# Row maxima of the attention taken from pairs of PSUM banks, in five groups per head group

## The chip, the cores and the metric

The kernel runs on one core of a Trainium2 chip. The metric is the device time of one execution in microseconds (us), the median of several runs. Engines: PE (TensorE, matrix products), DVE (VectorE), ACT (ScalarE), POOL (GpSimd), SP (SyncE, issues DMAs).

## The reference

The reference is a small network on 4096 tokens (8 sequences of 512) with 256 channels: two convolution-like blocks, an attention (L2), a mixture of experts, a second attention (L3) with rotary positions and gates, and a second mixture of experts. The change touches only the core that both attentions share. In the reference it is, for 16 query heads, 4 key/value heads and a head size of 16:

```python
scores = jnp.einsum('bgrqd,bgkd->bgrqk', qg, k) * SCALE       # r: 4 heads share one k, v
scores = jnp.where(causal, jnp.finfo(scores.dtype).min, scores)
attn = jax.nn.softmax(scores, axis=-1)
out = jnp.einsum('bgrqk,bgkd->bgrqd', attn, v)
```

In L3 the result is also multiplied by a gate per token and head. A softmax subtracts the largest score of each row (query) before the exponential.

## The kernel before

`attention` (from L1171) works through 32 units u per layer, one for each of 8 sequences and 4 key/value heads. A unit has 4 heads of 512 queries by 512 keys, causal, so in blocks of 128 a head has 10 blocks of scores; 4 heads are 40 blocks, or ten PSUM banks of 512 columns. The ten banks are the list `order`, n = 0 to 9, in the kinds A, B, A, B, C, A, B, A, B, C. Each unit passes two times over its scores:

- Maxima, two units ahead. PE computes scores with the queries on the partitions into `ps_m` (`max_unit`, L1299): A is one query block against 512 keys, B one against 384 and one against 128, C two against 256; each piece is a bf16 product (L1310) and a 128x128 product that adds the causal mask (L1312). DVE takes the row maxima (`reduce`, L1436: A at L1443, B at L1445 and L1446, C at L1448). `ps_m` has two banks, n%2, so bank n waits until the maxima of n-2 have been taken (`m_reduced`).
- `turn_tops` (L1331): one PE transpose turns the 16 columns of maxima into `ps_top`; DVE splits them in two bf16 parts (`split_tops`, L1457 and L1459), and SP puts them as two more rows below the queries (`put_tops`, L1243), so that the second product subtracts them.
- Exponentials. PE computes the scores again with the keys on the partitions into the two banks of `ps_t` (`exp_unit`, L1327), bank n waits for the exponential of n-2; ACT takes the exponential (L1403). POOL clears what lies above the diagonal when all ten are there (four selects, L1273).
- `weigh_values` (L1348), one unit later: probabilities by values, in four key blocks kb, into `ps_v`. ACT copies the sums (`copy_out`, L1410). `turn_out` (L1358), another unit later: four transposes into `ps_o`, from which DVE divides by the sum of the row (`normalise`, from L1468; L3 has one multiply by the gate more, L1471).

PE's instructions stand in one order written by hand, in `unit` (L1361). For each n of unit u: `max_unit` of unit u+2, `exp_unit` of unit u; then at n=0 `turn_tops` of u+1, at n=3 (`TURN_AT`) `turn_out` of u-2, and at n = 4, 6, 8, 9 (`WEIGH_AT`) one key block of `weigh_values` of u-1. DVE has its own order in its `unit` (L1479): ten reductions of unit u+2, `split_tops` of u+1 after n=1, `normalise` of u-2 after n=4. Units 0 and 1 have their maxima ahead of all that; units 30 and 31 have none to take for later ones. The eight PSUM banks are `ps_m` 2, `ps_t` 2, `ps_v` 2 (by turns), `ps_o` 1, `ps_top` 1.

Of the kernel before, what the change touches and what calls it, by code (L numbers as in the profile page):

```python
# [15 lines left out]
F32 = mybir.dt.float32  # L16
# [1154 lines left out]
def attention(net, layer, weights, scratch, values, gates, out):  # L1171
# [13 lines left out]
    TURN_AT, WEIGH_AT = 3, (4, 6, 8, 9)  # L1185
    with ExitStack() as ctx:
# [36 lines left out]
        with nc.Block() as block:  # L1223
# [71 lines left out]
            def _(pe):  # L1295
# [3 lines left out]
                def max_unit(u, j, n, first):  # L1299

                    kind, r = order[n]
                    if n == 0:
                        pe.wait_ge(loaded[j], (u - j) * 24 + 96)
                    if not (first and n < 2):
                        pe.wait_ge(m_reduced, u * UN + n - 1)
                    bank = ps_m[:, n % 2, :]
                    pieces = {"A": [(r, 3, 0)], "B": [(r, 2, 0), (r, 0, 3 * P)], "C": [(r, 1, 0), (r + 1, 1, 2 * P)]}
                    for head, qb, at in pieces[kind]:
# [5 lines left out]
                    last.then_inc(m_scored, 1)  # L1314
# [16 lines left out]
                def turn_tops(u, j):  # L1331
                    pe.wait_ge(m_reduced, u * UN + UN)
                    pe.transpose(ps_top[0:GR * TB, 0:P], top[j % 2][:, :, :].rearrange("p h t -> p (h t)"),
                                 net.ident[:, :]).then_inc(top_turned, 1)

                def weigh_values(u, j, kb, first):

                    if kb == 0:
                        pe.wait_ge(probs_ready, u + 1)
                        pe.wait_ge(v_ready, u + 1)  # L1340
                        if not first:
                            pe.wait_ge(oT_ready, u - 1)
                    pr = probs[j % 2]
                    for r in range(GR):
# [3 lines left out]
                        last = pe.matmul(ps_v[32 * r:32 * r + 32, j % 2, kb * P:S], v[j][:, kb, :], src,  # L1348
# [12 lines left out]
                def unit(u, j, maxima=True, tops=True, weigh=True, turn=True, first=False, first_turn=False,  # L1361
# [3 lines left out]
                    for n in range(UN):  # L1365
                        if maxima:
                            max_unit(u + 2, (j + 2) % 4, n, False)
                        exp_unit(u, j, n, first)
                        if n == 0 and tops:
                            turn_tops(u + 1, (j + 1) % 4)  # L1370
                        if n == TURN_AT and turn:
                            turn_out(u - 2, (j + 2) % 4, first_turn)
                        if n in WEIGH_AT and weigh:
                            weigh_values(u - 1, (j + 3) % 4, WEIGH_AT.index(n), first_weigh)
                for u in range(2):
                    for n in range(UN):
                        max_unit(u, u, n, u == 0)
                    if u == 0:
                        turn_tops(0, 0)
                unit(0, 0, weigh=False, turn=False, first=True)  # L1380
                unit(1, 1, turn=False, first_weigh=True)
                unit(2, 2, first_turn=True, first_weigh=True)
# [14 lines left out]
            def _(act):  # L1397
# [8 lines left out]
                def copy_out(u, j, first):  # L1406
# [3 lines left out]
                    act.activation(oT[j % 2][:, :], ps_v[:, j % 2, :], ACT.Copy).then_inc(oT_ready, 1)  # L1410
# [14 lines left out]
            def _(dve):  # L1425
# [10 lines left out]
                def reduce(u, j, n, first):  # L1436
                    kind, r = order[n]
                    if n == 0 and not first:
                        dve.wait_ge(top_turned, u - 1)
                    dve.wait_ge(m_scored, u * UN + n + 1)  # L1440
                    bank, t = ps_m[:, n % 2, :], top[j % 2]
                    if kind == "A":
                        last = dve.tensor_reduce(t[:, r, 3:4], bank, AX.X, ALU.max)  # L1443
                    elif kind == "B":
                        dve.tensor_reduce(t[:, r, 2:3], bank[:, 0:3 * P], AX.X, ALU.max)  # L1445
                        last = dve.tensor_reduce(t[:, r, 0:1], bank[:, 3 * P:4 * P], AX.X, ALU.max)  # L1446
                    else:
                        last = dve.tensor_reduce(t[:, r:r + 2, 1], bank.rearrange("p (h k) -> p h k", h=2),  # L1448
# [1550 lines left out]
```

## Time and profile before

| | |
|---|---|
| Time, 3 runs | 2412.57, 2414.94, 2416.8 us; median 2414.94 |
| Span of the profiled execution | 2414.8 us (the profile gives no other time of it) |
| PE busy | 2096.5 us (87%) |
| DVE busy | 1678.3 us (69%) |
| ACT busy | 1283.7 us (53%) |
| POOL busy | 711.2 us (29%) |
| Attention core of L2, first product to last unit | 387.4 to about 705 us |
| Attention core of L3, first product to last unit | 1464.0 to about 1782 us |

The span runs from the first to the last instruction. A matmul's duration in the trace holds the time in which its result runs through the array after its columns have gone in, so successive matmuls overlap in the rows, and the engine looks busy in small gaps. Where a difference of start times of two rows is used, it is the time that PE needed from one to the other.

### The profile page before, as it was taken

How to read it: one execution, taken by the hardware profiler on the slowest of the kernel's cores; microseconds unless marked ns; L12 is line 12 of the kernel's file. 1: busy time of each engine (PE TensorE's matmuls, PEld its weight loads, DVE VectorE, ACT ScalarE, POOL GpSimd, SP SyncE). 2: the span in 40 equal slices, each digit the busy share in tenths (PEclk: the TensorE clock that was granted, in tenths of full speed). 3: DMA queues.
4: the chain of work that ended last, by engine and by line, in shares of the span. 5: the costliest groups of instructions: out<-in, count | busy, mean ns of one | idle time of the engine just before them, and what ended most of it. 6: DMA issues, size and time to landing. Idle time of an engine off the chain costs nothing. (4 is left out here: it accounts for less than half of the span.)

```text
span 2414.8 us, 45217 instructions
## 1 busy us (share of the span) xinstructions
PE 2096.5 (87%) x15328; PEld 1597.7 (66%) x15328; DVE 1678.3 (69%) x3514; ACT 1283.7 (53%) x2221; POOL 711.2 (29%) x688
## 2 busy tenths in 40 slices
PE   5969777999987899959998467999985499999998
PEld 4758533444445788859998223444454399999998
DVE  2867756888845776636665697888835877777775
ACT  2434443666653444235554233666652088888885
POOL 1423200222220000038887000222210045555553
PEclk7989887999998899969999786999997799999999
DMA  3000033212103000086665342212104367777774
GB/s 123 1 0 0 0 84 101 59 51 56 51 9 108 3 1 1 1 198 117 116 98 70 102 106 75 59 50 56 51 1 110 123 207 220 222 222 223 222 224 97
DMA packets 176774, 218.56 MB, mean 91 GB/s; under 512 B 34057, under 2 KB 152498, under 8 KB 176242
## 3 DMA queue, kind: packets, MB, share of 16 engines
q1 hardware_dynamic: 146290, 175.19, 23.6%
q0 software_dynamic: 30336, 41.44, 10.7%
q8 instruction: 88, 1.44, 0.3%
q14 instruction: 60, 0.49, 0.1%
HBM read 161.25 MB, written 54.79 MB: 89 GB/s over the span
## 5 line engine op out<-in xcount | busy, mean ns | idle before, releaser
L1403 ACT ACTIVATE L_attn_probs<-L_attn_ps_t 128x512 f32<-128x512 f32 x640 | 374.8, 598 | 245.1 <-PE L_attn_ps_t L1327 240.0
L1310 PE MATMUL L_attn_ps_m<-L_attn_k,L_attn_q 96*128 96x512 bf16 (+3 forms) x1024 | 283.4, 316 | 35.3 <-DMA L_attn_k<-L_k_parts 28.7
L1273 POOL TENSOR_SCALAR_AFFINE_SELECT L_attn_probs<-L_attn_probs 128x512 f32<-128x512 f32 x256 | 153.3, 635 | 469.0 <-ACT L_attn_probs L1403 469.0
L1310 PEld LDWEIGHTS L_attn_ps_m<-L_attn_k,L_attn_q 96*128 96x128 bf16 x1024 | 101.8, 99 | 240.6 <-issue 71.8
L1327 PE MATMUL L_attn_ps_t<-L_attn_q,L_attn_k 98*128 98x512 bf16 (+3 forms) x1024 | 245.0, 301 | 2.8 <-ACT L_attn_probs L1403 2.3
L2450 POOL DMA_INDIRECT out<-L_experts_result,L_moe_give x78 | 161.7, 2073 | 208.6 <-DVE L_experts_result L2622 196.8
L1443 DVE TENSOR_REDUCE L_attn_top<-L_attn_ps_m 128x1 f32<-128x512 f32 x256 | 175.3, 685 | 61.8 <-PE L_attn_ps_m L1312 60.6
L1312 PE MATMUL L_attn_ps_m<-L_attn_causal,L_attn_ident 128*128 128x128 bf16 x1024 | 200.6, 227 | 0.0
L1348 PE MATMUL L_attn_ps_v<-L_attn_probs,L_attn_v 128*32 128x512 f32 (+3 forms) x2048 | 191.4, 448 | 3.0 <-POOL L_attn_probs L1273 2.8
L2729 POOL DMA_INDIRECT L_experts_token<-L_moe_rows,L_moe_take x80 | 81.8, 1022 | 377.7 <-POOLq L1766 324.0
L2468 PE MATMUL L_experts_ps_y<-L_experts_w_high,L_experts_hT_low 128*128 128x256 f32 x624 | 179.5, 288 | 0.0
L2468 PE MATMUL L_experts_ps_h<-L_experts_xT_high,L_experts_w_low 128*128 128x256 f32 x624 | 177.8, 285 | 0.0
L2469 PE MATMUL L_experts_ps_h<-L_experts_xT_high,L_experts_w_high 128*128 128x256 f32 x624 | 177.6, 285 | 0.0
L2470 PE MATMUL L_experts_ps_h<-L_experts_xT_low,L_experts_w_high 128*128 128x256 f32 x624 | 177.5, 284 | 0.0
L2470 PE MATMUL L_experts_ps_y<-L_experts_w_low,L_experts_hT_high 128*128 128x256 f32 x624 | 176.4, 283 | 0.0
L2469 PE MATMUL L_experts_ps_y<-L_experts_w_high,L_experts_hT_high 128*128 128x256 f32 x624 | 176.3, 283 | 0.0
L2556 ACT ACTIVATE L_experts_full<-L_experts_ps_h,L_staged_b 128x256 f32<-128x256 f32 x312 | 129.9, 467 | 68.3 <-PE L_experts_ps_h L2470 68.3
L2607 DVE TENSOR_TENSOR L_experts_hT_low<-L_experts_full,L_experts_hT_high 128x512 fp32r<-128x512 f32 x156 | 107.5, 690 | 67.9 <-ACT L_experts_hT_high L2561 42.3
L1445 DVE TENSOR_REDUCE L_attn_top<-L_attn_ps_m 128x1 f32<-128x384 f32 x256 | 140.2, 547 | 3.7 <-PE L_attn_ps_m L1312 2.7
L2438 POOL DMA_INDIRECT L_experts_token<-L_moe_rows,L_moe_take x78 | 90.4, 1160 | 168.2 <-POOLq L1766 144.7
L2739 POOL DMA_INDIRECT L_moe_total<-L_experts_result,L_moe_give x80 | 128.1, 1601 | 37.4 <-DVE L_experts_result L2907 23.9
L2894 DVE TENSOR_TENSOR L_experts_hT_low<-L_experts_full,L_experts_hT_high 128x256 fp32r<-128x256 f32 x160 | 64.5, 424 | 84.8 <-ACT L_experts_hT_high L2854 59.5
(435 smaller groups left out, 6110.5 us busy)
## 6 DMA issues: line engine op xcount, KB each, us to landing
L_staged_w<-L_ffn_w SPq DMA_DIRECT2D x78, 1024.0 KB, 6.6
L_attn_q<-L_q_parts SPq DMA_DIRECT2D x64, 192.0 KB
L_attn_q<-L_q_parts SPq DMA_DIRECT2D x64, 128.0 KB
L_moe_rows<-L_moe_ln_normed SPq DMA_DIRECT2D x16, 512.0 KB, 3.0
L_q_parts<-L_qkv_q_parts SPq DMA_DIRECT2D x32, 192.0 KB, 2.9
L_q_parts<-L_qkv_parts SPq DMA_DIRECT2D x32, 192.0 KB, 3.1
load_ring<-x SPq DMA_DIRECT2D x8, 512.0 KB, 4.2
L_attn_q<-L_q_parts SPq DMA_DIRECT2D x64, 64.0 KB
```

The source lines that it names most:

```text
L1273: return pool.affine_select(out=block, in_=block, compare_op=ALU.is_ge, fill=0.0, base=0, pattern=columns, channel_multiplier=-1)
L1310: pe.matmul(bank[:, at:at + width], q[j][0:96, head, qb * P:(qb + 1) * P], k[j][0:96, 0:width], start=True, stop=False)
L1312: last = pe.matmul(bank[:, at + width - P:at + width], ident16[:, :], causal16[:, :], start=False, stop=True)
L1327: last = pe.matmul(bank[:, at:at + width], k[j][0:98, kb * P:(kb + 1) * P], q[j][0:98, head, kb * P:S], start=True, stop=True)
L1348: last = pe.matmul(ps_v[32 * r:32 * r + 32, j % 2, kb * P:S], v[j][:, kb, :], src, start=kb == 0, stop=kb == TB - 1, tile_position=(0, 32 ...
L1403: act.activation(probs[j % 2][:, place[unit], :], ps_t[:, n % 2, :], ACT.Exp, scale=scale).then_inc(exped, 1)
L1443: last = dve.tensor_reduce(t[:, r, 3:4], bank, AX.X, ALU.max)
L1445: dve.tensor_reduce(t[:, r, 2:3], bank[:, 0:3 * P], AX.X, ALU.max)
L2450: pool.indirect_dma_start(out=total, out_offset=bass.IndirectOffsetOnAxis(ap=tables.give[:, t:t + 1], axis=0), in_=result[t % GIVEN][:, :] ...
L2468: pe.matmul(out, left_low, right_high, start=first, stop=False)
L2469: pe.matmul(out, left_high, right_high, start=False, stop=False)
L2470: return pe.matmul(out, left_high, right_low, start=False, stop=last)
```

## The change

The ten banks of maxima of a unit become five groups of two banks, the list `sweeps`: two A, two B (of heads 0 and 1), two C, two A, two B. `ps_m` has four banks in two pairs, used in turn. PE still scores one bank at each n (`max_bank`: group n//2, half n%2), but asks only at the first half of a group for the maxima of the group before last. DVE has one reduction over both banks for a group of kind A or C and two for kind B: 7 instead of 14 for a unit. The banks come from `ps_v`, which keeps one (so that `weigh_values` waits for the copy of the unit before, `oT_ready` u instead of u-1), and from `ps_top`, which becomes the first 16 partitions of the first quarter of `ps_o`. Since the two share a bank, `turn_tops` waits also for `normalise` (`o_done`), and `turn_out` for `split_tops` (`top_ready`). On PE `turn_tops` moves from n=0 to n=2 and `turn_out` from n=3 to n=5, behind the first key block of `weigh_values` at n=4. On DVE `split_tops` comes after group 1 and `normalise` after group 3.

```diff
+    sweeps = [[[(0, 3, 0)], [(1, 3, 0)]],
+              [[(0, 2, 0), (0, 0, 3 * P)], [(1, 2, 0), (1, 0, 3 * P)]],
+              [[(0, 1, 0), (1, 1, 2 * P)], [(2, 1, 0), (3, 1, 2 * P)]],
+              [[(2, 3, 0)], [(3, 3, 0)]],
+              [[(2, 2, 0), (2, 0, 3 * P)], [(3, 2, 0), (3, 0, 3 * P)]]]
+    SW = len(sweeps)
+    TOPS_AT, TURN_AT, WEIGH_AT = 2, 5, (4, 6, 8, 9)
...
-        ps_m = net.ps(f"{tag}_ps_m", [P, 2, S], F32, ctx)
+        ps_m = net.ps(f"{tag}_ps_m", [P, 2, 2, S], F32, ctx)
         ps_t = net.ps(f"{tag}_ps_t", [P, 2, S], F32, ctx)
-        ps_v = net.ps(f"{tag}_ps_v", [P, 2, S], F32, ctx)
+        ps_v = net.ps(f"{tag}_ps_v", [P, S], F32, ctx)
         ps_o = net.ps(f"{tag}_ps_o", [P, TB, P], F32, ctx)
-        ps_top = net.ps(f"{tag}_ps_top", [P, S], F32, ctx)
+        ps_top = ps_o[0:GR * TB, 0, :]
...
-                def max_unit(u, j, n, first):
-
-                    kind, r = order[n]
-                    if n == 0:
+                def max_bank(u, j, n, half, first):
+
+                    if n == 0 and half == 0:
                         pe.wait_ge(loaded[j], (u - j) * 24 + 96)
-                    if not (first and n < 2):
-                        pe.wait_ge(m_reduced, u * UN + n - 1)
-                    bank = ps_m[:, n % 2, :]
-                    pieces = {"A": [(r, 3, 0)], "B": [(r, 2, 0), (r, 0, 3 * P)], "C": [(r, 1, 0), (r + 1, 1, 2 * P)]}
-                    for head, qb, at in pieces[kind]:
+                    if half == 0 and not (first and n < 2):
+                        pe.wait_ge(m_reduced, u * SW + n - 1)
+                    bank = ps_m[:, (j + n) % 2, half, :]
+                    for head, qb, at in sweeps[n][half]:
                         width = (qb + 1) * P
                         pe.matmul(bank[:, at:at + width], q[j][0:96, head, qb * P:(qb + 1) * P], k[j][0:96, 0:width],
                                   start=True, stop=False)
                         last = pe.matmul(bank[:, at + width - P:at + width], ident16[:, :], causal16[:, :],
                                          start=False, stop=True)
-                    last.then_inc(m_scored, 1)
+                    if half:
+                        last.then_inc(m_scored, 1)
...
-                def turn_tops(u, j):
-                    pe.wait_ge(m_reduced, u * UN + UN)
-                    pe.transpose(ps_top[0:GR * TB, 0:P], top[j % 2][:, :, :].rearrange("p h t -> p (h t)"),
+                def turn_tops(u, j, first):
+
+                    pe.wait_ge(m_reduced, u * SW + SW)
+                    if not first:
+                        pe.wait_ge(o_done, u - 3)
+                    pe.transpose(ps_top, top[j % 2][:, :, :].rearrange("p h t -> p (h t)"),
                                  net.ident[:, :]).then_inc(top_turned, 1)
...
-                            pe.wait_ge(oT_ready, u - 1)
+                            pe.wait_ge(oT_ready, u)
...
-                def turn_out(u, j, first):
+                def turn_out(u, j, tops=True):
+
                     pe.wait_ge(oT_ready, u + 1)
-                    if not first:
+                    if tops:
+                        pe.wait_ge(top_ready, u + 4)
+                    else:
                         pe.wait_ge(o_done, u)
...
-                            max_unit(u + 2, (j + 2) % 4, n, False)
+                            max_bank(u + 2, (j + 2) % 4, n // 2, n % 2, False)
                         exp_unit(u, j, n, first)
-                        if n == 0 and tops:
-                            turn_tops(u + 1, (j + 1) % 4)
+                        if n == TOPS_AT and tops:
+                            turn_tops(u + 1, (j + 1) % 4, first_tops)
                         if n == TURN_AT and turn:
-                            turn_out(u - 2, (j + 2) % 4, first_turn)
+                            turn_out(u - 2, (j + 2) % 4, tops)
                         if n in WEIGH_AT and weigh:
...
                 def reduce(u, j, n, first):
-                    kind, r = order[n]
+
                     if n == 0 and not first:
                         dve.wait_ge(top_turned, u - 1)
-                    dve.wait_ge(m_scored, u * UN + n + 1)
-                    bank, t = ps_m[:, n % 2, :], top[j % 2]
-                    if kind == "A":
-                        last = dve.tensor_reduce(t[:, r, 3:4], bank, AX.X, ALU.max)
-                    elif kind == "B":
-                        dve.tensor_reduce(t[:, r, 2:3], bank[:, 0:3 * P], AX.X, ALU.max)
-                        last = dve.tensor_reduce(t[:, r, 0:1], bank[:, 3 * P:4 * P], AX.X, ALU.max)
+                    dve.wait_ge(m_scored, u * SW + n + 1)
+                    banks, t = ps_m[:, (j + n) % 2, :, :], top[j % 2]
+                    head, block, _ = sweeps[n][0][0]
+                    if block == 3:
+                        last = dve.tensor_reduce(t[:, head:head + 2, 3], banks, AX.X, ALU.max)
+                    elif block == 2:
+                        dve.tensor_reduce(t[:, head:head + 2, 2], banks[:, :, 0:3 * P], AX.X, ALU.max)
+                        last = dve.tensor_reduce(t[:, head:head + 2, 0], banks[:, :, 3 * P:4 * P], AX.X, ALU.max)
                     else:
-                        last = dve.tensor_reduce(t[:, r:r + 2, 1], bank.rearrange("p (h k) -> p h k", h=2),
+                        last = dve.tensor_reduce(t[:, :, 1], banks.rearrange("p b (h k) -> p (b h) k", h=2),
                                                  AX.X, ALU.max)
                     last.then_inc(m_reduced, 1)
...
-                    for n in range(UN):
+                    for n in range(SW):
                         if maxima:
                             reduce(u + 2, (j + 2) % 4, n, False)
                         if n == 1 and tops:
                             split_tops(u + 1, (j + 1) % 4, first_tops)
-                        if n == TURN_AT + 1 and turn:
+                        if n == 3 and turn:
```

## Rows read from the trace of the kernel before

**Rows 1.** Busy time by stretch: length, PE, PEld, DVE, ACT, POOL, granted clock, DMA.

```profile
430.00:680.00 250.00, 248.38 (x2265) 120.45 (x2261) 206.34 (x480) 166.33 (x294) 69.60 (x135) 1.00 0.20 52
```

**Rows 2.** Timeline, PE, turn_tops of units 1 and 29: start us, duration us.

```profile
412.88 0.28 PE L1333 MATMUL L_attn_ps_top<-ident,L_attn_top 128*16 128x128 f32 x1
...
676.48 0.27 PE L1333 MATMUL L_attn_ps_top<-ident,L_attn_top 128*16 128x128 f32 x1
...
1490.17 0.28 PE L1333 MATMUL L_attn_ps_top<-ident,L_attn_top 128*16 128x128 f32 x1
...
1753.76 0.27 PE L1333 MATMUL L_attn_ps_top<-ident,L_attn_top 128*16 128x128 f32 x1
```

**Rows 3.** Timeline, PE, one period of the L2 attention from turn_out on.

```profile
499.64 0.60 PE L1358 MATMUL L_attn_ps_o<-ident,L_attn_oT 128*128 128x128 f32 x4
500.17 0.28 PE L1310 MATMUL L_attn_ps_m<-L_attn_k,L_attn_q 96*128 96x256 bf16 x1
...
500.83 1.06 PE L1348 MATMUL L_attn_ps_v<-L_attn_probs,L_attn_v 128*32 128x512 f32 x8
...
502.12 0.38 PE L1327 MATMUL L_attn_ps_t<-L_attn_q,L_attn_k 98*128 98x512 bf16 x1
502.33 0.33 PE L1310 MATMUL L_attn_ps_m<-L_attn_k,L_attn_q 96*128 96x384 bf16 x1
...
503.77 0.39 PE L1310 MATMUL L_attn_ps_m<-L_attn_k,L_attn_q 96*128 96x512 bf16 x1
...
505.85 0.38 PE L1327 MATMUL L_attn_ps_t<-L_attn_q,L_attn_k 98*128 98x256 bf16 x2
...
506.52 0.39 PE L1310 MATMUL L_attn_ps_m<-L_attn_k,L_attn_q 96*128 96x512 bf16 x1
...
507.02 0.27 PE L1333 MATMUL L_attn_ps_top<-ident,L_attn_top 128*16 128x128 f32 x1
...
507.47 0.38 PE L1327 MATMUL L_attn_ps_t<-L_attn_q,L_attn_k 98*128 98x384 bf16 x2
507.75 0.39 PE L1310 MATMUL L_attn_ps_m<-L_attn_k,L_attn_q 96*128 96x512 bf16 x1
...
508.04 0.38 PE L1327 MATMUL L_attn_ps_t<-L_attn_q,L_attn_k 98*128 98x512 bf16 x1
508.48 0.34 PE L1310 MATMUL L_attn_ps_m<-L_attn_k,L_attn_q 96*128 96x384 bf16 x1
```

**Rows 4.** Timeline, DVE, the same period; idle time and its releaser in brackets.

```profile
500.04 0.54 DVE L1445 TENSOR_REDUCE L_attn_top<-L_attn_ps_m 128x1 f32<-128x384 f32 x1
500.50 0.27 DVE L1446 TENSOR_REDUCE L_attn_top<-L_attn_ps_m 128x1 f32<-128x128 f32 x1
500.72 0.69 DVE L1448 TENSOR_REDUCE L_attn_top<-L_attn_ps_m 128x2 f32<-128x512 f32 x1
501.32 0.25 DVE L1468 RECIPROCAL L_attn_inv<-L_attn_ps_o 128x16 f32<-128x16 f32 x1
...
507.00 0.69 DVE L1443 TENSOR_REDUCE L_attn_top<-L_attn_ps_m 128x1 f32<-128x512 f32 x1 [0.26 <-PE L_attn_ps_m L1312]
...
508.15 0.28 DVE L1446 TENSOR_REDUCE L_attn_top<-L_attn_ps_m 128x1 f32<-128x128 f32 x1
```

**Rows 5.** Timeline, DVE, normalise in the L3 attention.

```profile
1606.86 0.25 DVE L1468 RECIPROCAL L_attn_inv<-L_attn_ps_o 128x16 f32<-128x16 f32 x1
1607.25 0.18 DVE L1471 TENSOR_TENSOR L_attn_inv<-L_attn_inv,L_gates 128x16 f32<-128x16 f32 x1
1607.58 0.42 DVE L1474 TENSOR_TENSOR L_heads<-L_attn_ps_o,L_attn_inv 128x256 f32 x1
1607.92 0.68 DVE L1443 TENSOR_REDUCE L_attn_top<-L_attn_ps_m 128x1 f32<-128x512 f32 x1
```

**Rows 6.** Groups by line and shape: count, busy us, mean ns, idle us before.

```profile
L893 DVE TENSOR_TENSOR L_qkv_q_rest<-L_qkv_ps_q,L_qkv_q_parts 128x1024 f32<-128x1024 f32 x8 | 9.8, 1224 | 19.5 <-ACT L_qkv_q_parts L859 19.5
```

**Rows 7.** Timeline, POOL's selects in the period of rows 3.

```profile
507.03 2.40 POOL L1273 TENSOR_SCALAR_AFFINE_SELECT L_attn_probs<-L_attn_probs 128x512 f32<-128x512 f32 x4 [6.83 <-ACT L_attn_probs L1403]
```

More of the change, by code:

```diff
@@ L1347, in weigh_values @@
                                3: pr[:, GR + r, 3 * P:4 * P]}[kb]
-                        last = pe.matmul(ps_v[32 * r:32 * r + 32, j % 2, kb * P:S], v[j][:, kb, :], src,
+                        last = pe.matmul(ps_v[32 * r:32 * r + 32, kb * P:S], v[j][:, kb, :], src,
                                          start=kb == 0, stop=kb == TB - 1, tile_position=(0, 32 * r))
@@ L1359, in turn_out, with unit @@
                     last.then_inc(o_turned, 1)
-                def unit(u, j, maxima=True, tops=True, weigh=True, turn=True, first=False, first_turn=False,
+                def unit(u, j, maxima=True, tops=True, weigh=True, turn=True, first=False, first_tops=False,
                          first_weigh=False):
@@ L1375, in _ @@
                 for u in range(2):
-                    for n in range(UN):
-                        max_unit(u, u, n, u == 0)
+                    for n in range(2 * SW):
+                        max_bank(u, u, n // 2, n % 2, u == 0)
                     if u == 0:
[L1379 to L1382, printed above, removed]
+                        turn_tops(0, 0, True)
+                unit(0, 0, weigh=False, turn=False, first=True, first_tops=True)
+                unit(1, 1, turn=False, first_tops=True, first_weigh=True)
+                unit(2, 2, first_tops=True)
                 unit(3, 3)
@@ L1409, in copy_out @@
                         act.wait_ge(o_turned, u - 1)
-                    act.activation(oT[j % 2][:, :], ps_v[:, j % 2, :], ACT.Copy).then_inc(oT_ready, 1)
+                    act.activation(oT[j % 2][:, :], ps_v[:, :], ACT.Copy).then_inc(oT_ready, 1)
                 exponentials(0, 0, True)
@@ L1455, in split_tops @@
                         dve.wait_ge(tops_in[(j + 2) % 4], (u - 2 - (j + 2) % 4) * 8 + 32)
-                    rows, src = top_rows[j % 2], ps_top[0:GR * TB, 0:P]
+                    rows, src = top_rows[j % 2], ps_top
                     dve.tensor_copy(rows[:, 0, :], src).then_inc(top_hi, 1)
@@ L1479, in unit @@
                 def unit(u, j, maxima=True, tops=True, turn=True, first_tops=False, first_norm=False):
-                    for n in range(UN):
+                    for n in range(SW):
                         if maxima:
@@ L1485, in unit @@
                             split_tops(u + 1, (j + 1) % 4, first_tops)
-                        if n == TURN_AT + 1 and turn:
+                        if n == 3 and turn:
                             normalise(u - 2, first_norm)
                 for u in range(2):
-                    for n in range(UN):
+                    for n in range(SW):
                         reduce(u, u, n, True)
```

1 line of the change is left out of this document (removed).

## The prediction

> **What bounds the kernel now.** I read the busy times by stretch first. In the middle of an attention PE is busy 248.38 of 250 us, at a granted clock of 1.00 (the upper level, 2.4 GHz), while DVE has 206 us [rows 1]. So PE sets the pace there, but a matmul's row is longer than the time until the next can start, and such rows hide small waits. I therefore read start times. The rows of `turn_tops` show a strict period: 28 units take 263.60 us in L2 and 263.59 us in L3, 9.41 us a unit in both, although L3's DVE does more [rows 2]. The rest of the network is not touched, so the question is what becomes of 9.41.
>
> Inside one period I compare start-to-start times of equal work on PE [rows 3]. A product of 512 columns lets the next start after 0.22 us (502.12 to 502.33). There are three places where it takes longer:
> - after `turn_out`: four transposes take 0.53 us (499.64 to 500.17). Their rows span 0.60 us together and one lasts 0.27, so three steps are 0.33, one 0.11, four 0.44. Lost: 0.09.
> - before the maxima of n=2: 0.28 us (507.47 to 507.75), also 512 columns. Lost: 0.06. The reduction of n=0 ends at 507.00+0.69 = 507.69 [rows 4], and PE goes on 0.06 later, which is the price of a handoff.
> - before the maxima of n=3: 0.44 us (508.04 to 508.48). Lost: 0.23. It is the bank of n=1, whose second reduction ends at 508.43 [rows 4].
>
> So PE waits 0.38 us a unit for maxima, and its own work is 9.41-0.38 = 9.03 us. DVE idles elsewhere (0.26 us before 507.00): the two wait for each other in turns, with two banks between them.
>
> **What the change does to these waits.** PE's products are the same, so 9.03 us stays the floor. The question is which of two closed chains becomes longer than that.
>
> Chain through POOL. `weigh_values` of a unit can start only when POOL has cleared its probabilities. From the last scores of n=9 to the end of POOL's four selects it is 505.85 to 507.03+2.40 = 509.43 [rows 3, 7], 3.58 us, and a handoff of 0.06. From the first product of values to the scores of n=9 PE needs 500.83 to 505.85 = 5.02 us [rows 3], without a wait in it. Before, `turn_out` stood ahead of this stretch; now, at n=5, it stands in it: +0.44. The chain is 3.58+0.06+5.02+0.44 = 9.10 us. Before the change it was 8.66 us and hidden. This is the price of moving `turn_out`: 0.07 us a unit over PE's floor.
>
> Chain through DVE. The bank pair of group 1 (n=2) is that of the last group's reductions of the unit before. PE's way from n=2 to n=7 is its period less the way from n=7 to n=2: 503.77 to 506.52 is 2.75, and n=0 and n=1 take 0.50 each (506.52 to 507.02) [rows 3]. So 9.03-3.75 = 5.28. From the start of a bank of kind A to its reduction it is 0.48 (506.52 to 507.00) [rows 3, 4]. Then DVE reduces group 3, does `normalise`, and reduces group 4 twice.
>
> No row shows a reduction over two banks. A DVE operation on 1024 columns that reads PSUM lasts 1.22 us [rows 6], one on 512 lasts 0.69 [rows 4]: 0.53 us for 512 more columns. I add that to the start-to-start time of 512, 0.60 us (500.72 to 501.32), and get 1.13 us for group 3; for group 4, 0.46 (500.04 to 500.50) + 384 columns at the same rate 0.40 = 0.86, and for the second, whose end is waited for, 0.27+0.13 = 0.40. Let x be what each of the three takes beyond this. The low end is x = -0.03 (the 0.22 us between 500.50 and 500.72 suggests a start that costs little), the high end x = 0.15: an operation's duration is some 0.15 us over its columns, and reading a second bank might pay that again. I take x = 0, because the row on 1024 columns is the nearest.
>
> `normalise` takes 1606.86 to 1607.92 = 1.06 us in L3, of which the multiply by the gates is 1607.25 to 1607.58 = 0.33 [rows 5]; so 0.73 in L2. The sum: handoff 0.06, PE 5.28, then 0.48, 1.13, 0.73, 0.86, 0.40: 8.94 us in L2. L3 has 0.33 more: 9.27 us.
>
> So L2 is bound by POOL at 9.10 us and L3 by DVE at 9.27 us a unit: 0.31 and 0.14 less than 9.41. In L2 PE waits for maxima no more and a little for POOL; in L3 it waits about 0.24 us before n=2.
>
> At this place a rule of the Trainium skill speaks against the change's gain. Its page "VectorE: DVE Perf Modes", section "The DRAIN you can't avoid", says that the next operation does not start until the pipeline of the one before is empty (though one that is not held starts earlier). By it whole durations would count; the rows here show the next start 0.08 us before the end (500.04+0.54 = 500.58 against 500.50) [rows 4], so the sum goes by start times, and the other way is a rival below.
>
> **What hides the other edits.** Half as many reductions save DVE seven starts a unit; beyond the chain above that is idle time. `turn_tops` at n=2: 1.0 us later than now, but the maxima that it needs are those that n=2 has already waited for, so no wait of its own. Its `o_done` was given a unit before. `turn_out` on `top_ready`: with n=0 as zero, n=3 starts at 1.67, its reduction at about 2.2, group 1 takes 0.86+0.34 and `split_tops` about 0.6, so 4.0; PE reaches `turn_out` at about 4.5. Cover 0.5 us in both layers (all shifts together in L3); without it every product behind it would be late, the scores of n=6 first. SP: its two DMAs for the top rows (issued in 1.2 us, landed after at most 3.2 us by the view of that line) are ready at about 4.1, landed by 8.5, and wanted at 9.4 by the first scores of the next unit; the loads before them are issued earlier and are not delayed. One bank for `ps_v`: ACT copies it in the first microsecond and a half of a unit, PE wants it at 3.4. ACT's exponentials have 6.2 of 9.4 us.
>
> **Ends.** Unit 1 has `weigh_values` but no `turn_out`: 9.41 becomes 9.10-0.44 = 8.66 in both layers, 0.75 each, 1.5 together. Units 0 and 1's maxima ahead of all run at 1.2 GHz (clock 0.50 in that stretch) and take 16.8 us in L2; two groups in flight with 1.2 us of PE, 0.35 handoff and 1.2 us of DVE give 2.8 us per two groups, about 15.8 us for both. Some is lost again, since the clock rises later in the work. I take 0.9 a layer: 1.8. Units 30 and 31 run at POOL's chain without maxima (7.1 us by ACT's rows); there `turn_out` was done while PE waited for POOL and now stands behind that wait: 0.44 for each, 1.8 us lost together.
>
> Sum: 28 x 0.31 = 8.7 in L2; 28 x 0.14 = 3.9 in L3; +1.5 +1.8 -1.8: 14.1 us. The span is 2414.8 and the median 2414.94; the page gives no other time of the profiled execution, and the two agree, so 2401.
>
> **Rivals.**
> - POOL bounds both layers. If x is -0.06, DVE's chain in L3 is 9.09 and both are at 9.10: 28 x 0.31 x 2 + 1.5 = 18.9, so 2396. For it: the short starts. Against: the row of 1024 columns.
> - The reductions do not overlap. Each of the three costs its duration: 1.22, 0.94 and 0.40, and x is 0.06 on average. L2 is then 9.11, L3 9.44: 28 x (0.30-0.03) + 1.5 = 9, so 2406. For it: the skill's rule named above. Against: the overlap in rows 4. The reductions may also overlap less over two banks.
> - Slower: each reduction pays the start again at its second bank, x = 0.15. L2 becomes 9.39, L3 9.72: PE waits for DVE before n=2 in every unit. 28 x (0.02-0.31) + 1.5 = -6.6, so 2421. It decides from x of about 0.11, where the two layers cancel. For it: nothing in this trace reads two banks with a pattern that jumps. Against: rows 6 read 1024 columns of PSUM at one start.
> - The waits only move. Then 9.41 stays, at 2414. For it: both layers have the same period with different DVE work. Against: the three gaps end with reductions of banks that are now given back earlier.
>
> **Chances.** The forecast 0.52, with its own range 2397 to 2405; POOL in both 0.12; no overlap 0.14; slower 0.12; waits only move 0.10. 0.2% is 4.8 us, about what a measurement of this kernel can tell from no change. Faster by more than that: 0.52+0.12+0.14 = 0.78; within it 0.11; slower 0.11. The range: 2393 to 2412 leaves out the slower case and little more.
>
> **What would show it.** In L2 the period of `turn_tops` is 9.10 and the gap before the first product of values is released by POOL; in L3 it is 9.27 and the gap of 0.2 stands before n=2's maxima, released by the last reduction. Reductions of 1024 columns last 1.22 us. Period 9.03 in L2 would show POOL's step too long by my sum; a period over 9.41 in L3 with x over 0.05 would show the DVE chain mis-sized; a wait at `turn_out` would show that `split_tops` comes late. If L3 gains as much as L2, the DVE chain was never last.

## The result

| | time, median (range) | ratio to before beside it |
|---|---|---|
| before | 2415.87 us (4 runs) | |
| changed | 2402.98 us (2392.48 to 2404.54, 4 runs) | 0.9933, interval 0.9914 to 0.9952 |
| changed, word for word again | 2399.47 us (2392.33 to 2406.53, 6 runs) | 0.9919, interval 0.9903 to 0.9935 |

Faster by 0.7%; 2401 was forecast. The profiled execution took 2402.66 us, with a span of 2401.0 against 2414.8. Runs of one kernel spread by some 10 us. The profiles show one reason: the stretches that no edit touches differ between profiles, the one between the attentions from 754 to 760 us and the one after the second from 629 to 633. Periods repeat to 0.01 us, so the reading goes by periods, and the times only have to agree with them.

The page of the changed kernel, span, busy times and the group of the two-bank reductions:

```profile
span 2401.0 us, 44539 instructions
...
PE 2084.7 (87%) x15328; PEld 1612.0 (67%) x15328; DVE 1642.8 (68%) x3066; ACT 1280.1 (53%) x2221; POOL 711.1 (30%) x688
...
L1455 DVE TENSOR_REDUCE L_attn_top<-L_attn_ps_m 128x2 f32<-128x1024 f32 x128 | 156.6, 1223 | 73.7 <-PE L_attn_ps_m L1316 71.5
```

A reduction over two banks lasts 1.22 us, as the sum had it. Busy time by stretch in the changed kernel (columns as in [rows 1]), a stretch of L2 and one of L3:

```profile
430.00:680.00 250.00, 249.10 (x2325) 127.26 (x2323) 194.38 (x300) 169.71 (x304) 69.88 (x137) 1.00 0.20 51
```

```profile
1510.00:1740.00 230.00, 227.39 (x2110) 115.14 (x2112) 180.92 (x298) 153.47 (x274) 64.48 (x125) 1.00 0.20 53
```

DVE has 12 us less in the stretch of L2 than before, PE still looks full, with 60 products more in the same 250 us. In L3 PE is idle 2.6 us of 230: there is a wait there that its long rows do not hide. Now the timeline of the changed kernel, PE, `turn_tops` of two units of L2 and two of L3 (the rows answering to [rows 2]):

```profile
428.80 0.28 PE L1341 MATMUL L_attn_ps_o<-ident,L_attn_top 128*16 128x128 f32 x1
...
665.09 0.27 PE L1341 MATMUL L_attn_ps_o<-ident,L_attn_top 128*16 128x128 f32 x1
...
1524.55 0.27 PE L1341 MATMUL L_attn_ps_o<-ident,L_attn_top 128*16 128x128 f32 x1
...
1738.23 0.27 PE L1341 MATMUL L_attn_ps_o<-ident,L_attn_top 128*16 128x128 f32 x1
```

26 units take 236.29 us in L2, 9.09 a unit; 23 take 213.68 in L3, 9.29 a unit. (The first few units of L3 take 9.10 to 9.12, while DVE still has a lead; so its mean is 9.27.) Before both were 9.41.

**L2, a period of the changed kernel.** The timeline of PE, from the last scores ahead of `weigh_values` on:

```profile
502.54 0.38 PE L1332 MATMUL L_attn_ps_t<-L_attn_q,L_attn_k 98*128 98x256 bf16 x2
502.88 1.06 PE L1356 MATMUL L_attn_ps_v<-L_attn_probs,L_attn_v 128*32 128x512 f32 x8
...
508.33 0.38 PE L1332 MATMUL L_attn_ps_t<-L_attn_q,L_attn_k 98*128 98x256 bf16 x2
```

and of POOL:

```profile
500.43 2.40 POOL L1279 TENSOR_SCALAR_AFFINE_SELECT L_attn_probs<-L_attn_probs 128x512 f32<-128x512 f32 x4 [6.51 <-ACT L_attn_probs L1414]
```

POOL ends at 502.83 and the products of values start at 502.88, 0.05 us later. They start 0.34 us after the scores before them, where it is 0.31 ahead of the other three key blocks (508.33 to 508.64): the wait is 0.03 us. The maxima have none left in L2. Not so in L3; the waits view of the changed kernel from 1530 to 1740, in total, times and longest:

```profile
PEld L_attn_ps_m L1314 <- DVE L_attn_top L1458: 8.9, 23, 0.4
```

It comes once a unit.

**L3, a period of the changed kernel.** The timeline of DVE and then of PE at the start of n=2:

```profile
1613.34 1.23 DVE L1455 TENSOR_REDUCE L_attn_top<-L_attn_ps_m 128x2 f32<-128x1024 f32 x1 [1.09 <-PE L_attn_ps_m L1316]
1614.48 0.25 DVE L1480 RECIPROCAL L_attn_inv<-L_attn_ps_o 128x16 f32<-128x16 f32 x1
...
1615.53 0.95 DVE L1457 TENSOR_REDUCE L_attn_top<-L_attn_ps_m 128x2 f32<-128x768 f32 x1
1616.39 0.42 DVE L1458 TENSOR_REDUCE L_attn_top<-L_attn_ps_m 128x2 f32<-128x256 f32 x1
```

```profile
1616.38 0.38 PE L1332 MATMUL L_attn_ps_t<-L_attn_q,L_attn_k 98*128 98x384 bf16 x2
1616.87 0.34 PE L1314 MATMUL L_attn_ps_m<-L_attn_k,L_attn_q 96*128 96x384 bf16 x1
```

The maxima of n=2 start 0.49 us after the scores before them, where 0.22 is the pace: PE waits 0.27 us, until 0.06 us after the last reduction's end (1616.39+0.42 = 1616.81).

**Where the 13.8 us of span come from.** Per layer, in profiles of both kernels. The head runs from the first product of maxima to the `turn_tops` in unit 1, the tail from that in unit 29 to the last product (both corrected for `turn_tops` standing 1.0 us later in a unit):

| us | L2 | L3 | forecast, each |
|---|---|---|---|
| head, to unit 1 | -2.4 | -3.0 | -0.9 |
| unit 1 | -0.5 | -0.6 | -0.75 |
| units 2 to 28 | -8.8 | -3.8 | 27 x 0.31 = -8.4, 27 x 0.14 = -3.8 |
| tail, unit 29 to the end | +2.1 | +1.6 | about +0.6, +0.8 |
| sum | -9.5 | -5.8 | |

Stretches outside, not edited: +1.1, +1.0, -0.7. Together -13.9.

The heads gained more because the granted clock rose earlier. The windows view of before and then of the changed kernel, the same 16 us of L2's head and the 4 us after it (the clock is the third number from the end):

```profile
388.00:404.00 16.00, 14.20 (x64) 5.86 (x61) 13.80 (x30) 0.00 (x0) 0.00 (x0) 0.50 0.26 69
404.00:408.00 4.00, 3.89 (x18) 2.24 (x19) 3.07 (x7) 1.68 (x3) 0.00 (x0) 0.50 0.01 2
```

```profile
388.00:404.00 16.00, 13.54 (x73) 7.66 (x72) 13.79 (x17) 1.19 (x2) 0.00 (x0) 0.61 0.26 69
404.00:408.00 4.00, 3.49 (x29) 2.16 (x28) 3.31 (x7) 3.40 (x6) 0.00 (x0) 0.98 0.01 1
```

The changed kernel is at 2.4 GHz in the last 4 us, before is at 1.2 GHz there. In the tails the clock went the other way: the changed kernel has 0.79 from 689 to 697, and its last 32 products of values take 4.06 us instead of 2.36.

### The profile page after: what moved, and what is told of

Same layout as the page of the kernel before. It is cut to its first block and busy times, and to the rows that moved or that the text cites. A ratio compares the mean times of both kernels' runs of the same rounds, so it can differ in the third digit from the quotient of the medians.

```text
span 2401.0 us, 44539 instructions
## 1 busy us (share of the span) xinstructions
PE 2084.7 (87%) x15328; PEld 1612.0 (67%) x15328; DVE 1642.8 (68%) x3066; ACT 1280.1 (53%) x2221; POOL 711.1 (30%) x688
## 5 line engine op out<-in xcount | busy, mean ns | idle before, releaser
L1314 PE MATMUL L_attn_ps_m<-L_attn_k,L_attn_q 96*128 96x512 bf16 (+3 forms) x1024 | 277.5, 312 | 35.0 <-DMA L_attn_k<-L_k_parts 29.3
L1455 DVE TENSOR_REDUCE L_attn_top<-L_attn_ps_m 128x2 f32<-128x1024 f32 x128 | 156.6, 1223 | 73.7 <-PE L_attn_ps_m L1316 71.5
L1457 DVE TENSOR_REDUCE L_attn_top<-L_attn_ps_m 128x2 f32<-128x768 f32 x128 | 122.2, 955 | 8.4 <-PE L_attn_ps_m L1316 3.0
L2480 PEld LDWEIGHTS L_experts_ps_h<-L_experts_xT_high,L_experts_w_low 128*128 128x128 f32 x624 | 120.8, 194 | 0.0
```

The source lines that it names most:

```text
L1314: pe.matmul(bank[:, at:at + width], q[j][0:96, head, qb * P:(qb + 1) * P], k[j][0:96, 0:width], start=True, stop=False)
L1455: last = dve.tensor_reduce(t[:, head:head + 2, 3], banks, AX.X, ALU.max)
L2480: pe.matmul(out, left_low, right_high, start=first, stop=False)
```

## The experiments

Each run stands beside the kernel before on its chip. Periods are the mean of the later 18 units of each layer in the profile, in us; times and ratios as above.

| kernel | L2 | L3 | time | ratio, interval |
|---|---|---|---|---|
| before | 9.41 | 9.41 | | |
| changed | 9.09 | 9.29 | 2402.98 | 0.9933, 0.9914 to 0.9952 |
| order only | 9.28 | 9.55 | 2416.58 | 1.0005, 0.9994 to 1.0016 |
| a reduction per bank | 9.16 | 9.48 | 2406.81 | 0.9970, 0.9956 to 0.9985 |
| `normalise` earlier | 9.09 | 9.09 | 2397.55 | 0.9915, 0.9883 to 0.9947 |
| four single banks | 9.09 | 9.09 | 2389.22 | 0.9896, 0.9868 to 0.9924 |
| three selects | 9.06 | 9.29 | 2392.74 | 0.9908, 0.9884 to 0.9933 |
| values later | 9.06 | 9.06 | 2388.58 | 0.9881, 0.9862 to 0.9900 |
| single banks, values later | 9.06 | 9.06 | 2388.46 | 0.9883, 0.9861 to 0.9905 |
| values in two runs | 9.04 | 9.04 | 2389.19 | 0.9883, 0.9858 to 0.9908 |
| second run last | 8.56 | 8.56 | 2353.61 | 0.9738, 0.9726 to 0.9751 |
| the same with groups | 8.57 | 8.80 | 2367.59 | 0.9803, 0.9788 to 0.9818 |

### A reduction per bank

The changed kernel with its pairs of banks and its order, but DVE reduces each bank by itself.

```diff
-                        last = dve.tensor_reduce(t[:, head:head + 2, 3], banks, AX.X, ALU.max)
+                        for h in range(2):
+                            last = dve.tensor_reduce(t[:, head + h, 3:4], banks[:, h, :], AX.X, ALU.max)
```

(and in the same way for B and C.)

> Same groups, pairs of banks and order as the changed kernel, but one reduction for each bank (14 a unit instead of 7). Theory (chain through VectorE: handoff, PE from n=2 to n=7, group 3, normalise, group 4): group 3 costs 0.60+0.60 instead of 1.13 us, group 4 0.46+0.22+0.46+0.28 instead of 0.86+0.40, together 0.23 us more. L2 goes from 8.94 to 9.17 us a unit and passes the chain through POOL (9.09 measured); L3 goes from the measured 9.29 to 9.52. 28 x 0.08 + 26 x 0.23 = 8 us more than the changed kernel: about 2411. Rival (the pairs of banks bring the gain and the number of reductions does not matter): periods stay 9.09 and 9.29, about 2403.

Measured: 9.16 and 9.48. DVE's timeline of this kernel in L3:

```profile
1614.46 1.29 DVE L1456 TENSOR_REDUCE L_attn_top<-L_attn_ps_m 128x1 f32<-128x512 f32 x2 [1.03 <-PE L_attn_ps_m L1316]
1615.67 0.25 DVE L1483 RECIPROCAL L_attn_inv<-L_attn_ps_o 128x16 f32<-128x16 f32 x1
...
1616.72 0.55 DVE L1459 TENSOR_REDUCE L_attn_top<-L_attn_ps_m 128x1 f32<-128x384 f32 x1
...
1617.85 0.28 DVE L1460 TENSOR_REDUCE L_attn_top<-L_attn_ps_m 128x1 f32<-128x128 f32 x1
```

Group 3 takes 1.21 us (1614.46 to 1615.67) instead of 1.14, group 4 to its end 1.41 instead of 1.28: 0.20 in the chain (0.23 was expected), and the period of L3 rose by 0.19. The time is 4 us under the expected 2411. So fewer reductions are worth what the chain holds of them, and no more. In L2 the period went from POOL's 9.09 to 9.16, which is DVE's chain there with 0.20 added: that chain, hidden in the changed kernel, is 8.96 us (8.94 by the prediction's sum).

### The order alone

The kernel before with `turn_tops` at n=2 and `turn_out` at n=5 (and DVE's two steps placed to match); banks and reductions as before.

```diff
-    TURN_AT, WEIGH_AT = 3, (4, 6, 8, 9)
+    TOPS_AT, TURN_AT, WEIGH_AT = 2, 5, (4, 6, 8, 9)
...
-                        if n == 0 and tops:
+                        if n == TOPS_AT and tops:
                             turn_tops(u + 1, (j + 1) % 4)
...
-                        if n == 1 and tops:
+                        if n == 3 and tops:
...
-                        if n == TURN_AT + 1 and turn:
+                        if n == 7 and turn:
```

> The kernel before with its banks and 14 reductions, but with the changed kernel's order: turn_tops at n=2, turn_out at n=5, split_tops after the reduction of n=3, normalise after that of n=7. Theory (the gain is in the banks of the maxima): with two single banks the two engines still wait for each other in turns, the period stays at 9.3 to 9.6 us in both layers and the time at 2412 to 2425. Rival (the order brings the gain): 9.1 in L2, 9.3 in L3, about 2403.

Measured: 9.28 in L2, 9.55 in L3, and no difference in time. The order helps one layer as much as it harms the other; the gain of the change is not the order's. The waits for single reductions are still there; a row of its waits view for L2 (430 to 660):

```profile
PEld L_attn_ps_m L1310 <- DVE L_attn_top L1446: 27.0, 72, 0.6
```

In the changed kernel no reduction stands in that view but once, with 0.2 us.

### Normalise one group earlier, and four single banks

Both take DVE's chain of L3 away by other means. The first moves `normalise` on DVE ahead of group 3, where DVE idled 1.09 us.

```diff
-                        if n == 3 and turn:
+                        if n == 2 and turn:
```

> The changed kernel with normalise on VectorE after group 2 instead of after group 3. Theory: the 1.06 us of normalise in L3 leave the VectorE chain and fall into an idle stretch of 1.09 us before group 3, so that chain is 8.23 us, and L3 goes from 9.29 to POOL's 9.09 us a unit; L2 stays at 9.09. 26 x 0.20 = 5.2 us less than the changed kernel, about 2398. Rival (L3's longer period comes from something else, the top rows' DMA or the handoffs): L3 stays at 9.29 and the time at 2403.

Measured: 9.09 in both layers. L3's 0.20 is gone, at no cost: `normalise` was on the chain only because it stood between the reductions of groups 3 and 4.

The second gives `ps_m`'s four banks one by one, with a reduction per bank as before.

```diff
-                    if half == 0 and not (first and n < 2):
-                        pe.wait_ge(m_reduced, u * SW + n - 1)
-                    bank = ps_m[:, (j + n) % 2, half, :]
+                    at = 2 * n + half
+                    if not (first and at < 4):
+                        pe.wait_ge(m_reduced, u * UN + at - 3)
+                    bank = ps_m[:, (j + n) % 2, half, :]
```

> The changed kernel with its four banks used one by one: VectorE starts on a bank as soon as it is scored, PE waits for the bank of n-4, 14 reductions a unit; split_tops and normalise stand at the same places (after n=3 and n=7). Theory (what counts is how far PE may run ahead, not how few reductions there are): normalise ends early enough for n=8's bank to be free 0.8 us before PE's n=2 and n=9's 0.9 us before n=3, so the VectorE chain is hidden in both layers and POOL's bounds both: 9.09 and 9.09 to 9.12. 26 x 0.19 = 5 us less than the changed kernel, about 2398. Rival (the merged reductions bring the gain): 9.2 or more in L2, 9.5 in L3, over 2410.

Measured: 9.09 in both layers, with twice as many reductions as in the changed kernel. A bank is asked for again when one reduction is done, not when a group is. Its heads are 3 us shorter too (21.1 us to unit 1 instead of 24.1), which the expectation left out; with the stretch between the attentions, which is 4.6 us shorter in this profile, they are why 2389 came out where 2398 was expected. Single banks are only part of the 3 us: from 12 to 17 us after the first product the granted clock is 1.00 in these heads and 0.50 in the changed kernel's, and two heads with groups whose clock is 1.00 there (in L3 of the runs with three selects and with groups at the end) take 23.3 and 22.7 us. So by these heads 1.6 to 2.2 us go with the banks and the rest with the clock. Word for word again on another chip, beside the changed kernel, also word for word:

> Four single banks in turn for the maxima (the experiment with one reduction per bank and the output sums' bank shared as before the earlier one), again word for word. If its lead over the changed kernel is its layer 3 period (9.09 instead of 9.29, 28 units: 5.6 us) and its shorter heads (3 us each), it is 8 to 14 us faster than the changed kernel on the same chip too; if the lead was the chip's, it is within 3 us of it.

> The changed kernel again, word for word, for its time beside the two others on one chip. Both theories: periods 9.09 (layer 2) and 9.27 to 9.29 us (layer 3), 2400 to 2405 and 0.5 to 0.8% less than the kernel before.

Measured: 2388.48 us (2382.73 to 2394.15) against 2399.47 (2392.33 to 2406.53): 11 us. The changed kernel's periods are 9.09 and 9.29 again.

### Is it POOL in L2?

One run has a select less, so that some probabilities above the diagonal stay in; otherwise it is the changed kernel:

```diff
-                        keep_causal(pr[:, GR:2 * GR, 0:P], [[0, GR], [1, P]])
```

> The changed kernel without one of POOL's four selects (the first query block of the second key block stays unmasked above the diagonal, so the sums differ from the reference). Theory: POOL's chain is 0.59 us shorter, 8.50; L2 falls from 9.09 to PE's 9.03 to 9.07; L3 is bound by VectorE and stays at 9.29. 1 to 2 us less than the changed kernel, about 2401. Rival (POOL bounds L3 as well, with VectorE only sharing the wait): L3 falls too, by 0.1 us or more a unit, under 2399.

Two more move `weigh_values` away from POOL's end, the first with groups and the earlier `normalise`, the second with four single banks:

```diff
-    TOPS_AT, TURN_AT, WEIGH_AT = 2, 5, (4, 6, 8, 9)
+    TOPS_AT, TURN_AT, WEIGH_AT = 2, 6, (5, 6, 8, 9)
```

> As the kernel with the earlier normalise, and weigh_values' first key block at n=5 instead of n=4, turn_out at n=6 behind it. Theory: the chain through POOL now has one step n less (0.56 us) and is 8.53 us, the chain through VectorE is 8.2 us or less, so both layers fall to PE's own work, 9.03 us (0.04 more where PE waits for ScalarE at n=2): 0.03 to 0.06 us less than 9.09 for each of 56 units, 2 to 3 us, about 2395. Rival (9.09 is not POOL's chain but PE's own work, with the sum of the pieces 0.06 too small): stays at 9.09, 2397.5.

> Four single banks, with weigh_values from n=5 and turn_out at n=6. Theory: neither chain reaches PE's own work: 9.03 to 9.06 us in both layers against 9.09 for four single banks alone, 2 to 3 us less, about 2387. Rival (the later values make ScalarE or the copy late and PE waits there): 9.09 or more, no gain.

Measured: 9.06 in L2 by each way, and the wait for POOL is in no row of their waits views of L2; L3 stays at 9.29 with three selects and goes to 9.06 where `normalise` is also earlier. So POOL's chain was last in L2 by 0.03 us. With groups and with single banks what comes next is the same 9.06, and it is not PE alone: the scores of n=2 wait 0.04 us for ACT, which copies the sums before it takes the unit's first exponential. ACT and PE with single banks and values later:

```profile
606.36 0.59 ACT L1421 ACTIVATE L_attn_oT<-L_attn_ps_v 128x512 f32<-128x512 f32 x1
606.83 0.61 ACT L1414 ACTIVATE L_attn_probs<-L_attn_ps_t 128x512 f32<-128x512 f32 x1
```

```profile
607.40 0.22 PE L1317 MATMUL L_attn_ps_m<-L_attn_causal,L_attn_ident 128*128 128x128 bf16 x1
607.50 0.39 PE L1332 MATMUL L_attn_ps_t<-L_attn_q,L_attn_k 98*128 98x512 bf16 x1
```

606.83+0.61 and a handoff of 0.06 make 607.50; behind such a 128-column product the pace is 0.06, here it is 0.10. PE's own work is therefore 9.02 us.

The times are 2389 for values later, 2388 for single banks with values later and 2393 for three selects, where about 2395, 2387 and 2401 were expected. With three selects the time lies under the bound of 2399 that the rival gave, but L3's period has not moved: by the profiles its tails are 2.6 and 3.9 us shorter than the changed kernel's (by the select or by the clock, which no run separates) and the stretch between the attentions 4.9. The differences in period, 1 to 2 us in all, are less than a run's spread.

### Values in two runs

The kernel with single banks and later values is the base from here on. PE's 9.06 contains four separate runs of fp32 products (`weigh_values`) among bf16 ones. Two key blocks at a time leave the products the same and halve the changes.

```diff
-    TOPS_AT, TURN_AT, WEIGH_AT = 2, 6, (5, 6, 8, 9)
+    TOPS_AT, TURN_AT, WEIGH_AT = 2, 6, {5: (0, 1), 8: (2, 3)}
```

> Four single banks, weigh_values in two runs: key blocks 0 and 1 at n=5, 2 and 3 at n=8, turn_out at n=6. In every trace so far PE loses 0.09 us on entering a key block's fp32 products and 0.10 us on leaving them, also where nothing is waited for. Theory: two entries fewer save 0.38 us of PE's own work, 8.65 us; but ScalarE needs 0.56 us for an exponential and PE 0.50 to 0.56 for a step, and ScalarE is idle in the longer runs, so PE will wait for it by about 0.3 us from n=2 on: 8.7 to 8.95 us, 6 to 19 us less than four banks with the values later, 2368 to 2381. Rival (the 0.19 us belong to the switch of each key block and not to the change of type): no gain, 9.05 or more.

Missed: 9.04, where 8.7 to 8.95 was expected. PE's work shrank, by 0.47 us where 0.38 was forecast (9.04 less waits of 0.08 and 0.41 for ACT is 8.55, against 9.02), but ACT, which already held PE for 0.04 us, took its place. PE's timeline of this kernel:

```profile
506.49 0.22 PE L1317 MATMUL L_attn_ps_m<-L_attn_causal,L_attn_ident 128*128 128x128 bf16 x1
506.95 0.39 PE L1332 MATMUL L_attn_ps_t<-L_attn_q,L_attn_k 98*128 98x512 bf16 x1 [0.25 <-ACT L_attn_probs L1414]
```

and ACT's:

```profile
505.32 0.60 ACT L1414 ACTIVATE L_attn_probs<-L_attn_ps_t 128x512 f32<-128x512 f32 x1 [0.85 <-PE L_attn_ps_t L1332]
505.81 0.59 ACT L1421 ACTIVATE L_attn_oT<-L_attn_ps_v 128x512 f32<-128x512 f32 x1
506.29 3.47 ACT L1414 ACTIVATE L_attn_probs<-L_attn_ps_t 128x512 f32<-128x512 f32 x6
...
511.41 0.60 ACT L1414 ACTIVATE L_attn_probs<-L_attn_ps_t 128x512 f32<-128x512 f32 x1 [1.64 <-PE L_attn_ps_t L1332]
```

ACT's copy of the output sums stands ahead of six exponentials in a row; PE, with two banks of scores, waits for them, and then ACT idles 1.64 us while PE multiplies values. ACT is busy 155.83 of 230 us (430 to 660), 6.1 of 9.04 a unit: it is the order in time that holds, not the amount.

### The second run last

```diff
-    TOPS_AT, TURN_AT, WEIGH_AT = 2, 6, {5: (0, 1), 8: (2, 3)}
+    TOPS_AT, TURN_AT, WEIGH_AT = 2, 6, {5: (0, 1), 9: (2, 3)}
```

> Four single banks for the maxima, the value products in two runs: key blocks 0 and 1 at n = 5, blocks 2 and 3 now at n = 9 instead of n = 8; turn_out at n = 6. With the second run at n = 8 the period was 9.04 us: ScalarE's copy of the output sums stood in front of the first exponentials of the next unit, exponential 2 began 0.25 us late and PE waited for its buffer. Theory (a): what is left in the period is ScalarE's queue, and only its order. One place later the copy falls where ScalarE idles for 1.64 us; exponential 2 is late by about 0.04 us and PE is bound by its own products, about 8.65 us. Period 8.65 to 8.75, 56 units by 0.3 us: 17 to 20 us less than with n = 8, about 2370. Rival (b): the end of the value products comes later by one block, so the copy and all behind it on ScalarE are later too, and PE waits as before: period 8.95 or more, about 2385.

Measured: 8.56 in both layers, 2353.61 us, 2.6% under the kernel before. ACT's timeline of this kernel:

```profile
504.83 0.60 ACT L1414 ACTIVATE L_attn_probs<-L_attn_ps_t 128x512 f32<-128x512 f32 x1 [1.65 <-PE L_attn_ps_t L1332]
505.77 1.72 ACT L1414 ACTIVATE L_attn_probs<-L_attn_ps_t 128x512 f32<-128x512 f32 x3 [0.34 <-PE L_attn_ps_t L1332]
507.79 0.60 ACT L1421 ACTIVATE L_attn_oT<-L_attn_ps_v 128x512 f32<-128x512 f32 x1 [0.30 <-PE L_attn_ps_v L1356]
```

ACT now takes the exponential of n=9 while PE multiplies the second run, so that only the copy stands between that run and the next unit's exponentials; with the run at n=8 both stood there (505.32 and 505.81). PE's wait at n=2 is down to 0.01 us, and PE is idle for 1.3 us of 230. Theory (a) holds in that the order of ACT's queue was all that was left, but not in the place: the idle 1.65 us where it saw the copy fall is still there, and the copy follows another one of 0.30 us. The time is 16 us less than it said. Two terms: the period is 0.49 us less and not 0.3, since PE's own work is 8.55 and not 8.65 (56 x 0.19 = 10); and the tails are 4.1 and 2.4 us shorter, in L2 mostly by the granted clock: 0.83 and 0.72 in the last units of L2 with the second run at n=8, 1.00 here.

### The same with groups

The fastest kernel with the changed kernel's groups of two banks in place of single banks, to see DVE's chain where PE no longer covers it.

> The changed kernel's groups of two banks (two pairs in turn), with the value products in two runs (key blocks 0 and 1 at n = 5, blocks 2 and 3 at n = 9), turn_out at n = 6 and the normalisation before group 3: all of the fastest kernel so far but its four single banks. In that kernel the period was 8.555 us in both layers, bound by PE. Theory (a): with groups the DVE's own chain shows again, now that PE is short enough: from the end of turn_out the normalisation (0.74 us from start to start in layer 2, 1.05 in layer 3), group 3's reduction (1.14), group 4's two (0.86 + 0.42), then PE's group 1, 0.06 later. Laid over the fastest kernel's PE sequence, this ends 0.06 us before PE wants the banks in layer 2 and 0.25 us after in layer 3. So 8.56 in layer 2, 8.81 in layer 3; with 3 us more in each head, 2353.6 + 28 by 0.25 + 6 = about 2367. Rival (b): the groups cost nothing in the period, as when it was 9.06: 8.56 in both layers, about 2360. Rival (c): two pairs in turn let PE run ahead less and the short stretches before values bunch up: 8.9 or more in both, 2375 or more.

Measured: 8.57 in L2, 8.80 in L3, 2367.59 us: the periods within 0.01 us of theory (a). That the time is within 1 us is partly luck: by their profiles the attentions take 3.6 and 6.3 us more than with single banks, 10 and not 13, and the stretch between them, which no edit touches, 4.3 more. DVE's timeline of this kernel in L3:

```profile
1595.87 0.26 DVE L1480 RECIPROCAL L_attn_inv<-L_attn_ps_o 128x16 f32<-128x16 f32 x1 [1.10 <-PE L_attn_ps_o L1369]
...
1596.93 1.22 DVE L1455 TENSOR_REDUCE L_attn_top<-L_attn_ps_m 128x2 f32<-128x1024 f32 x1
1598.06 0.95 DVE L1457 TENSOR_REDUCE L_attn_top<-L_attn_ps_m 128x2 f32<-128x768 f32 x1
1598.93 0.42 DVE L1458 TENSOR_REDUCE L_attn_top<-L_attn_ps_m 128x2 f32<-128x256 f32 x1
```

and PE's, where the maxima of n=2 start 0.41 us after the scores before them instead of 0.22:

```profile
1598.99 0.38 PE L1332 MATMUL L_attn_ps_t<-L_attn_q,L_attn_k 98*128 98x384 bf16 x2
1599.40 0.34 PE L1314 MATMUL L_attn_ps_m<-L_attn_k,L_attn_q 96*128 96x384 bf16 x1
```

1598.93+0.42+0.06 = 1599.41. Groups cost 10 us here against single banks, by the same means as in the changed kernel: 0.24 us in each period of L3, and 3.0 and 1.6 us in the heads.

## Why the prediction was right

**The two chains.** L2 by POOL: forecast 9.10, measured 9.09. Its terms one by one: scores of n=9 to POOL's end 3.59 (forecast 3.58; 499.24, one period ahead of 508.33, to 502.83), handoff 0.05 (0.06), first values to scores of n=9 with `turn_out` in between 5.45 (5.02+0.44). L3 by DVE: forecast 9.27, measured 9.29: PE's way from n=2 to n=7 5.27 (5.28; 1607.58 to 1612.85), from there to its reduction 0.49 (0.48), group 3 1.14 (1.13), `normalise` 1.05 (1.06), group 4 0.86 and 0.42 (0.86, 0.40), handoff 0.06. Each chain was then moved by itself: a select less moves L2 alone, an earlier `normalise` L3 alone. That is shown, not only argued.

**x is zero.** The three reductions take 1.14, 0.86 and 0.42 us in the chain, 0.03 us over the sum together. The slower rival (x = 0.15) falls with it, and so does the rival without overlap: the second reduction of group 4 starts at 1616.39, while the first ends at 1615.53+0.95 = 1616.48. The page "VectorE: DVE Perf Modes" of the Trainium skill, section "The DRAIN you can't avoid", has the next operation wait until the pipeline is empty, but lets one that is not held start earlier; this trace shows the earlier start, by 0.09 us, over two banks as over one.

**The floor.** PE's own work was put at 9.03 us; the runs show 9.02. But no kernel ran at it: ACT's copy and first exponential hold PE for 0.04 us and make 9.06 the lowest period until the values go into two runs. The prediction counted ACT's busy time and its copy as covered and left this third chain out. It changed nothing here, since both its chains were above 9.06.

**The ends.** The tails' mechanism was right: the exponentials of a last unit take 7.51 us instead of 7.10 in L2, 0.41 more for each of two units (0.44 forecast). The size of the ends was off in three terms that nearly cancel: heads 2.4 and 3.0 instead of 0.9, because the clock rose within them; tails 1.5 and 0.8 us worse than said, because the clock fell within them; unit 1 gained 0.5 and not 0.75. That the time came within 2 us of the forecast is partly luck for that reason; the periods did not need it. Why the clock rises or falls there is open: no run varied it alone.

**The side conditions.** No row shows a wait at `turn_out` or for the one bank of output sums, as said.

The rival of POOL in both layers (2396) was the result of a later run, `normalise` earlier: 9.09 in both and 2397.55. What neither forecast nor rivals saw is that the change's two parts work against each other: the extra PSUM banks bring the gain, and pairing them gives 5.6 us back in L3's period, as long as `normalise` stands between groups 3 and 4, and 1.6 to 2.2 of the 3 us in each head.

## What to carry to other kernels

Write down each closed chain of a loop, engine by engine, with start-to-start times, and compare it with the period: the change in time is that of the longest chain, and a cheaper operation on another chain is worth nothing. More buffers help by how early a single one comes free, so try single banks in turn before grouping them to save instructions. When the bounding engine's own work shrinks, look at the order of the others' queues next; one place later for one run of products took 0.49 us off each period here, 27 of the 33 us between the spans (2384.8 to 2351.9).

## What the hardware showed unexpectedly

- A run of the fp32 products of `weigh_values` costs about 0.25 us beyond its products. Four key blocks taken one at a time take 1.00, 0.79, 0.58 and 0.36 us until the next product starts, 2.73 together (502.88 to 503.88 and so on in the changed kernel); in two runs 1.64+0.78 = 2.42. And the scores ahead of each run take 0.31 us where 0.22 is their pace. Two runs fewer save 0.31+0.18 = 0.49 us, which is, within 0.02, the step from 9.02 to 8.55 in PE's own work. The rows of the fastest kernel:

```profile
502.18 0.38 PE L1332 MATMUL L_attn_ps_t<-L_attn_q,L_attn_k 98*128 98x512 bf16 x1
502.49 1.71 PE L1356 MATMUL L_attn_ps_v<-L_attn_probs,L_attn_v 128*32 128x512 f32 x16
504.13 0.39 PE L1315 MATMUL L_attn_ps_m<-L_attn_k,L_attn_q 96*128 96x512 bf16 x1
...
504.42 0.38 PE L1332 MATMUL L_attn_ps_t<-L_attn_q,L_attn_k 98*128 98x384 bf16 x2
504.63 0.60 PE L1369 MATMUL L_attn_ps_o<-ident,L_attn_oT 128*128 128x128 f32 x4
505.08 0.38 PE L1315 MATMUL L_attn_ps_m<-L_attn_k,L_attn_q 96*128 96x512 bf16 x1
```

It is not the change of type as such: the last three rows are four fp32 transposes among the same bf16 products, and they start 0.21 us after the scores before them, without the extra 0.09, and take 0.45, about four steps of 0.11. With single banks and values later, where values follow the transposes, the same four take 0.53, so the entry costs 0.09 us there too, from fp32 to fp32:

```profile
602.05 0.60 PE L1369 MATMUL L_attn_ps_o<-ident,L_attn_oT 128*128 128x128 f32 x4
602.58 0.85 PE L1356 MATMUL L_attn_ps_v<-L_attn_probs,L_attn_v 128*32 128x384 f32 x8
```

What in these products costs it, no run shows.

- Handoffs are alike over engines here: 0.06 us from a reduction's end to PE's next product, 0.05 from POOL's.
- The granted clock in a head or tail differs between kernels that differ only in order or banks: 0.50 against 0.61 and 0.98 in L2's head, 0.72 against 1.00 in its tail; in the changed kernel it was worth 0.8 to 2.1 us each time. The order is not the only cause: two profiles of the same code, four single banks, have 1.00 and 0.66 in L3's head from 12 to 17 us after the first product.
